# Masked query copies of a causal linear attention: from four ScalarE copies to one VectorE product

## What is computed

```python
q_phi = jax.nn.elu(q) + 1.0
k_phi = jax.nn.elu(k) + 1.0
kv_prefix = jnp.cumsum(k_phi[..., :, None] * v[..., None, :], axis=1)
k_prefix = jnp.cumsum(k_phi, axis=1)
num = jnp.einsum('bthd,bthdm->bthm', q_phi, kv_prefix)
denom = jnp.sum(q_phi * k_prefix, axis=-1, keepdims=True)
attn = num / (denom + 1e-06)
```

## Time and profile before

| | us |
|---|---|
| median of 3 runs | 5524.06 |
| lowest and highest | 5520.37, 5528.53 |
| the profiled execution | 5523.19 |
| its span | 5521.5 |

### The profile page before, as it was taken

The page is one execution under the profiler, slowest core; times in us unless marked ns, Lnnn a source line. Parts: engine busy times, 40 slices in busy tenths (PEclk is TensorE's granted clock), DMA queues, the critical chain, the costliest instruction groups (busy, mean ns, idle before and its releaser), DMA issues. The chain is left out here.

```text
span 5521.5 us, 148534 instructions
## 1 busy us (share of the span) xinstructions
PE 4891.5 (89%) x42260; PEld 4068.6 (74%) x42260; DVE 4018.0 (73%) x11109; ACT 3813.8 (69%) x12437; POOL 2456.8 (44%) x3763
## 2 busy tenths in 40 slices
PE   5996959996199997999889998899989999799994
PEld 3555948985178886888778887788867888688873
DVE  4554766777678876888768887788867888688875
ACT  1333423342189995999869997799968999599982
POOL 0000000000456664666636665566636666366661
PEclk7996969998599999999999999999999999999997
DMA  0001200000111111111111111111111111111111
GB/s 21 0 0 35 57 1 1 0 0 1 45 29 25 25 37 39 24 24 25 51 25 25 25 25 47 29 25 25 25 45 29 25 25 26 53 23 25 25 49 29
DMA packets 103071, 144.74 MB, mean 26 GB/s; under 512 B 65245, under 2 KB 72690, under 8 KB 102386
## 3 DMA queue, kind: packets, MB, share of 16 engines
q1 hardware_dynamic: 93410, 107.27, 8.6%
q0 software_dynamic: 9232, 33.12, 1.9%
HBM read 49.13 MB, written 2.10 MB: 9 GB/s over the span
## 5 line engine op out<-in xcount | busy, mean ns | idle before, releaser
L2036 ACT ACTIVATE d_probs<-d_S_ps,d_neg_max 128x96 f32<-128x96 f32 x3072 | 1003.0, 342 | 35.3 <-issue 23.0
L1637 POOL TENSOR_TENSOR d_qk<-d_qk,d_sin_terms 128x512 f32<-128x512 f32 x768 | 961.2, 1273 | 29.9 <-DVE d_sin_terms L2223 29.9
L1812 PEld LDWEIGHTS d_S_ps<-d_kT,d_q_blocks 128*128 128x128 f32 x6144 | 791.0, 192 | 2.3
L1812 PE MATMUL d_S_ps<-d_kT,d_q_blocks 128*128 128x96 f32 x6144 | 790.1, 272 | 0.0
L2223 DVE TENSOR_TENSOR d_qk<-d_A_ps,d_tables 128x512 f32<-128x512 f32 x768 | 527.8, 687 | 232.8 <-ACT d_squares L1992 166.0
L2036 ACT ACTIVATION_READ_ACCUMULATOR d_probs<-d_S_ps,d_neg_max 128x1 f32 x3072 | 638.6, 208 | 0.0
L1769 PE MATMUL d_A_ps<-d_wqkv_hi,d_xT_hi 128*128 128x512 f32 x1152 | 558.6, 485 | 19.3 <-DVE d_sin_terms L2223 14.6
L1992 ACT ACTIVATE d_squares<-d_A_ps 128x512 f32<-128x512 f32 x768 | 462.4, 602 | 125.9 <-PE d_A_ps L1771 125.4
L2223 DVE TENSOR_TENSOR d_sin_terms<-d_A_ps,d_tables 128x512 f32<-128x512 f32 x768 | 523.0, 681 | 0.0
L2044 ACT ACTIVATE d_probsT<-d_PT_ps 96x512 f32<-96x512 f32 (+1 forms) x768 | 460.3, 599 | 80.5 <-PE d_PT_ps L1822 80.3
L1776 PE MATMUL d_T_ps<-d_ident,d_qk 128*128 128x128 f32 x3072 | 483.2, 280 | 33.1 <-POOL d_qk L1674 29.1
(11 more groups left out here) (406 smaller groups left out, 10801.4 us busy)
## 6 DMA issues: line engine op xcount, KB each, us to landing
d_v_early<-d_v SPq DMA_DIRECT2D x192, 256.0 KB, 2.9
d_v_early<-d_v SPq DMA_DIRECT2D x192, 128.0 KB, 2.3
d_tables<-L_ffn_rotary POOLq DMA_DIRECT2D x7, 2048.0 KB, 8.4
d_qk<-L_ffn_Wqkv POOLq DMA_DIRECT2D x21, 512.0 KB, 3.9
d_xs<-d_xb SPq DMA_DIRECT2D x56, 127.0 KB
d_xs<-d_xb SPq DMA_DIRECT2D x96, 63.5 KB
ax_fp_blocks<-L_ffn_blocks_gu SPq DMA_DIRECT2D x16, 256.0 KB, 3.9
ax_fp_scales<-L_ffn_scales_gu SPq DMA_DIRECT2D x64, 64.0 KB, 3.4
```

The lines of the kernel that those rows point to most:

```text
L1637: nc.gpsimd.tensor_tensor(c4[:, :, s, :], c4[:, :, s, :], s4[:, :, 1 - s, :], ALU.add).then_inc(rotated, 1)
L1812: last = nc.tensor.matmul(S[g % 2][:, n * SEEN:(n + 1) * SEEN], qx[:, p, half, :], kT[b][jj][:, p, HALF * half:HALF * half + SEEN], start= ...
L2036: nc.scalar.activation(pr[:, g, n, seen_columns(g)], S[g % 2][:, n * SEEN:(n + 1) * SEEN], ACT.Exp, bias=nmax[:, g, n:n + 1], accum_out=de ...
```

## The change

ScalarE's four query copies and their function go. VectorE gets `query_heads`: one product of 128 x 512, whose first operand is the 128 columns of queries in the bank, read four times, and whose second is the four columns of `head4`, each repeated over 128 columns. It stands behind the cosines and ahead of the denominators. It waits for the transposes and for the four key copies of its step. `qx_ready` now rises by one in a step in place of four, and TensorE's two waits for it are changed to match.

```diff
@@ transpose_phi, TensorE
-                            pe.wait_ge(qx_ready, u * 4)
+                            pe.wait_ge(qx_ready, u)
@@ products, TensorE
-                        pe.wait_ge(qx_ready, u * 4 + 4)
+                        pe.wait_ge(qx_ready, u + 1)
@@ ScalarE
-                    def copy_q_heads(u, b):
-                        act.wait_ge(qkT_ps, u + 1)
-                        for h in range(4):
-                            nc.scalar.activation(qx[:, b, h, :], T_b[:, 0:P], ACT.Identity, scale=head4[:, h:h + 1]
-                                                 ).then_inc(qx_ready, 1)
@@ step, ScalarE
                         gate_tanh(u, b)
-                        copy_q_heads(u, b)
                         copy_k(u, b)
@@ VectorE
+                    def query_heads(u, b):
+                        v.wait_ge(qkT_ps, u + 1)
+                        v.wait_ge(kx_ready, u * 4 + 4)
+                        nc.vector.tensor_tensor(qx[:, b], T_b[:, 0:P].unsqueeze(1).broadcast_to([P, 4, P]),
+                                                head4[:].unsqueeze(2).broadcast_to([P, 4, P]), ALU.mult).then_inc(qx_ready, 1)
@@ step, VectorE
                         if not last:
                             cosines(u + 1, j1, 1 - b)
+                        query_heads(u, b)
                         if not first:
                             denominators(u - 1)
```

## The result

| | before | changed |
|---|---|---|
| median of 6 runs each, us | 5530.49 | 5548.34 |
| lowest and highest | 5520.37, 5535.84 | 5545.89, 5555.31 |
| ratio | | 1.0036, 95% interval 1.0023 to 1.0049 |
| profiled execution, its span | 5523.19, 5521.5 | 5555.31, 5553.6 |

The forecast was 5514.8 with a range of 5508 to 5526. The change costs 18 us by the medians; the two profiled executions lie 32 us apart. In a later comparison on one chip the same two kernels gave 5526.8 and 5554.8, ratio 1.0052 (1.0036 to 1.0067).

A forecast was written before the change was run, and what follows sets the result against it. In the TensorE-bound attention block, the stall (0.94 us a step) before the score matmul, awaiting ScalarE's key copies, was taken as the limit. 32 x 0.32 = 10.2 us less 1.0 for the clock gave 5514.8, range 5508 to 5526.

The forecast's parts named there:

- The step: Attention block: the first score matmul starts 0.32 us earlier in each of 32 steps, 9.57 us in place of 9.89.
- Start of the key copies: Attention step: without the query copies, ScalarE's key copies start 1.02 us earlier, 0.04 us after the transposes.
- hand-over to VectorE: Attention step: from the end of the key copies to the start of VectorE's product, 0.04 us, with 0.16 as the end.
- The estimate by the Trainium skill: Attention step: 0.63 us of ScalarE copies removed against 0.66 of VectorE product put in; no gain, about 5525.
- Later stages are as before, but meet the low stretches at other places.: Everything behind the attention block: no change in the stages themselves, 2 to 3 us allowed either way.
- gives back 1.0 us: Attention block: TensorE's low-clock stretches, covering less stall, take 1.0 us back from the 10.2 us gained.
- eight and a quarter less: Attention block: eight low-clock stretches cost 0.18 us more each, 1.4; a quarter of one less is met, 0.4.
- Slower: the clock: Rival, attention block: less idle TensorE gets the low clock more often; plus some 22 us, 5546; chance 0.03.
- the 0.95 that I had named as a sign of being wrong: Attention block: a granted TensorE clock below 0.95 would make the prediction wrong.
- Released sooner: Rival, attention step: the score matmul is handed over in 0.07 us, gaining 13.4 us: 5510.7; chance 0.17.
- dear product: Rival, attention step: VectorE's product takes 1.12 us, the score matmul starts 0.23 late; plus 7.4, 5531.5; chance 0.09.
- The chance of 0.05 for slower by over 0.2%: Whole kernel: chance 0.05 of a time above 5535.1 us, against 0.24 for faster by more and 0.71 within.

The follow-up runs named there:

- before_short16: Kernel before, FP4-stage layer-norm tiles copied by ScalarE in pairs, each raising its semaphore by one, ScalarE's stream 16 instructions shorter: 5547.7 us, ratio 1.0033.
- after_again: The changed kernel, unchanged, run again for a second trace on the chip of the others: 5554.8 us (4 runs).
- before_again: The kernel before, unchanged, run again for a second trace: 5527.4 us (10 runs), ratio 1.0001.
- after_pad16: The changed kernel with 16 one-column copies at the head of ScalarE's part of the attention block: 5529.9 us, ratio 1.0004.
- before_longer: The kernel before with two more, unused, query copies on ScalarE ahead of its four in each step: 5595.6 us (one run).
- qbank_pad16: The changed kernel with 16 padding copies on ScalarE and the query transposes in the output projection's bank: 5488.6 us, ratio 0.9924 against the kernel before.
- qbank_late: qbank_pad16 with an unused 128x512 VectorE product ahead of the query product, bringing back a short stall: 5496.1 us (one run).

## Why the prediction was wrong

**The step was right.** Start of the key copies 0.04 us behind the transposes (forecast 0.04), product 0.69 (0.69), hand-over to VectorE 0.03 (0.04), to TensorE 0.23 (0.20), step 9.60 (9.57). The estimate by the Trainium skill, "Perfetto Trace Analysis", section "Optimizing Scalar/DVE Operations", that was weighed against it did not hold for ScalarE: the trace has the copies at 1.02 us, not at 0.63. For the product it was near: 0.69 us against 0.66.

**Failed: "Later stages are as before, but meet the low stretches at other places."** This carries 25 of the 32 us between the profiled executions, and all of the 18 by the medians (before_short16, which has the shift without the change: 18 us). What failed is the term put at nothing for ScalarE's loops behind the block; in its place came 20 us of idle, 0.57 in each of 36 turns. I had counted the instructions that the edit takes out of ScalarE's queue as time, and not as 16 instructions fewer ahead of every later loop. I also allowed only 2 to 3 us for anything behind the block, without a row for it. The row was there: 23.0 us of "issue" ahead of d_probs before, 36 times.

**Failed in size: the low clock "gives back 1.0 us".** It gave back all of the 9 (319.4 us in after_again, 319.6 in before_again). The cost of one long step was near (1.5 to 1.7 us against 1.6), and that each would cost somewhat more than before was right; their number was taken as fixed in time, eight and a quarter less, and there were 11 of 29 in place of 7. Four more of 1.6 and 7 times 0.2 make 7.8 us of the 8.1 that 29 steps of 0.28 had gained; the first two steps gained nothing (23.3 us in both later traces). Why their number rises stays open.

**The rivals.** "Slower: the clock" had the right mechanism for the block: 0.93 granted in place of 0.96, below the 0.95 that I had named as a sign of being wrong. Its argument against, that the rhythm is the same through the stage, held for one step length only. It was not the reason for the total. "Released sooner" and "dear product" did not happen. No rival was about the layers. The chance of 0.05 for slower by over 0.2% was worked out from the block alone.

**Without the shift** the change makes no difference: after_pad16, 1.0004 (0.9995 to 1.0012).

## What to carry to other kernels

Read the stage you edit and the rest of the program apart: if a loop that you haven't touched takes longer per turn, look at the idle time marked "issue" behind its branch, and try a handful of idle instructions ahead of it, on the engine in question, before you judge the edit. A timed comparison of two versions with different instruction counts can be off by 0.3% and up to 3.4% here by that alone. In a block that TensorE bounds, shortening a repeated stall may give nothing until it is much shorter or gone; here moving one operand to a bank of its own removed it and, with the fillers on ScalarE, gained 0.76% over the kernel before.

## What was not expected of the hardware

- Where a loop lies in an engine's instruction stream sets what a turn costs: on ScalarE 0.57 us more of idle in each of 36 turns for 16 instructions fewer ahead of it (none for 8 fewer), on VectorE 3.7 us more for 10 instructions more (none for 6), with 508 loads of instructions in place of 328. The load that goes with ScalarE's stream starts 3.8 to 3.5 us ahead of the branch in the kernel before and 0.38 to 0.69 behind it in the kernels with the loss.
- The clock of TensorE went to its lower level (0.50, 1.2 GHz, as in the earlier trace rows) for short stretches in a block where it was busy over 90% of the time, with a stall in each step ahead of them, and did not do so where the stall was gone (mean 1.00 from 125 to 385 us, against 0.96, 0.93 and, with a stall of 1.4 us in before_longer, 0.84). The Trainium skill, "TensorE: Matmul & The Clock Gate", section "A second HAM failure mode: psum-queue depth-cycling", tells of a kernel in which short idle times between groups of matmuls make the clock swing between the two levels; these runs agree (0.96, 0.93 and 0.84 with a stall in each step, 1.00 without). A shorter stall (0.65 us) has more low stretches than a longer one (0.94), and why it is so stays open.
- Whether the clock starts late in the block isn't fixed: the first two steps took 27.3 us in one trace of the changed kernel and 23.3 in the other, and 26.4 and 26.7 in those of qbank_pad16 and qbank_late. This wasn't followed up.
